# Attention sums moved by DMA in the projection's layout, instead of transposed on TensorE

## The reference

```python
scores = jnp.einsum('bhid,bhjd->bhij', q, k) * scale        # 16 heads of 16 features
scores = jnp.where(causal, -jnp.inf, scores)
attn = jax.nn.softmax(scores, axis=-1)
out = jnp.einsum('bhij,bhjd->bhid', attn, v)
out = jnp.transpose(out, (0, 2, 1, 3)).reshape(b, n, d)
return out @ proj_w.T + proj_b
...
x = x + _layernorm(_L0_attn_ref(_layernorm(x, axis=-1), ...), axis=-1)
x = x + _layernorm(_L0_ffn_ref(_layernorm(x, axis=-1), ...), axis=-1)
```

## Time and profile before

| | us |
|---|---|
| median of 3 runs | 1443.12 (1441.19 to 1446.45) |
| the profiled execution's own time | 1444.75 |
| span of its instructions | 1442.9 |
| PE busy | 1320.8 (92%) |
| DVE busy | 1070.2 (74%) |
| ACT busy | 872.5 (60%) |
| POOL busy | 603.3 (42%) |
| mean granted TensorE clock | 0.957 |

### The profile page before, as it was taken

The page is one execution under the profiler, slowest core; times in us unless marked ns, Lnnn a source line. Parts: engine busy times, 40 slices in busy tenths (PEclk is TensorE's granted clock), DMA queues, the critical chain, the costliest instruction groups (busy, mean ns, idle before and its releaser), DMA issues.

```text
span 1442.9 us, 30280 instructions
## 1 busy us (share of the span) xinstructions
PE 1320.8 (92%) x12592; PEld 609.8 (42%) x12592; DVE 1070.2 (74%) x1800; ACT 872.5 (60%) x1200; POOL 603.3 (42%) x521
## 2 busy tenths in 40 slices
PE   4678999999999999999999999999999989999994
PEld 1323444444444444444444444444444433555441
DVE  4765777867777786877687778777788986647778
ACT  3214766657665766676677667766666767665451
POOL 5556482226534462446245634553411323222334
PEclk9768999989999999999999999999999999999997
DMA  4382453344435353544353435353454530212112
GB/s 157 100 148 91 75 122 87 60 91 75 104 60 119 68 111 61 119 76 104 60 119 75 104 60 120 75 105 60 93 72 61 108 91 2 74 48 84 59 45 101
DMA packets 79805, 124.21 MB, mean 86 GB/s; under 512 B 14006, under 2 KB 49972, under 8 KB 79668
## 3 DMA queue, kind: packets, MB, share of 16 engines
q1 hardware_dynamic: 79668, 122.28, 39.8%
HBM read 70.85 MB, written 50.33 MB: 84 GB/s over the span
## 4 chain that ended last, share of the span: by engine, by line
PE 65%; POOL 12%; ACT 9%; DVE 6%; issue 4%; DMA 3%; SPq 2%; DVEq 0%; ACTq 0%; POOLq 0%
PE PV L993 15%; PE RING L953 10%; PE RING L979 10%; ACT PB L1334 6%; PE MI L918 6%; PE RING L1051 4%; PE MI L1017 4%; POOL TA L749 2%; PE MI L928 2%; POOL TB L751 2%; PE RING L1044 2%; PE RING L1045 2%; PE RING L1035 2%; POOL PB L1404 2%; PE RING L960 2%
## 5 line engine op out<-in xcount | busy, mean ns | idle before, releaser
L1334 ACT ACTIVATE PB<-RING 128x1024 f32<-128x1024 f32 (+2 forms) x640 | 581.9, 939 | 291.7 <-PE RING L979 287.8
L1127 DVE TENSOR_REDUCE M<-RING 128x2 f32<-128x1024 f32 (+3 forms) x448 | 499.2, 1143 | 146.6 <-PE RING L960 73.1
L993 PE MATMUL PV<-PB,V 128*17 128x512 f32 (+3 forms) x3072 | 328.8, 507 | 6.8 <-POOL PB L1404 5.9
L953 PE MATMUL RING<-QK 48*128 48x512 f32 (+3 forms) x1536 | 300.2, 410 | 36.5 <-DVE M L1127 15.0
L1404 POOL TENSOR_SCALAR_AFFINE_SELECT PB<-PB 128x512 f32<-128x512 f32 x256 | 163.3, 641 | 390.4 <-ACT PB L1334 390.2
L979 PE MATMUL RING<-QK 50*128 50x512 f32 (+3 forms) x1536 | 280.7, 406 | 11.6 <-ACT PB L1334 7.0
L1127 DVE TENSOR_REDUCE MB<-RING 128x2 f32<-128x768 f32 (+2 forms) x192 | 197.4, 1042 | 70.9 <-PE RING L960 69.8
L953 PEld LDWEIGHTS RING<-QK 48*128 48x128 f32 x1536 | 149.1, 192 | 188.7 <-issue 65.4
L979 PEld LDWEIGHTS RING<-QK 50*128 50x128 f32 x1536 | 134.2, 189 | 175.7 <-ACT PB L1334 73.4
L960 PE MATMUL RING<-MASKK,MASKQ 64*128 64x64 bf16 x2048 | 122.7, 200 | 0.0
L918 PE MATMUL MI<-XT,WQ 128*32 128x512 f32 x896 | 114.4, 630 | 2.3 <-ACT EO L1307 1.6
(11 more groups left out here) (111 smaller groups left out, 1386.5 us busy)
## 6 DMA issues: line engine op xcount, KB each, us to landing
QK<-split_parts SPq DMA_DIRECT2D x372, 128.0 KB, 5.8
split_parts<-PARTS SPq DMA_DIRECT2D x64, 256.0 KB, 3.5
split_parts<-EO SPq DMA_DIRECT2D x64, 256.0 KB, 4.3
block_mid<-Y SPq DMA_DIRECT2D x16, 512.0 KB, 4.1
F_X<-block_mid SPq DMA_DIRECT2D x16, 512.0 KB, 5.7
X<-x SPq DMA_DIRECT2D x7, 1024.0 KB, 9.7
out<-F_Y SPq DMA_DIRECT2D x14, 512.0 KB, 2.9
QK<-NSROW SPq DMA_DIRECT2D x128, 8.0 KB, 1.9
```

Source lines behind the costliest of these rows:

```text
L953: ins = e.matmul(m[:, h, i, :], QK[g % 3][r, 0, k, 128 * t:128 * t + 128], QK[g % 3][r, 1, k, k0:k0 + n], start=True, stop=not open_end(g, s))
L993: ins = e.matmul(PV[32 * h:32 * h + 17, off:512], V[b % 2][:, j, 4 * (g % 4) + h, :], PB[(SLOTS * g + s) % 4][:, h, 0:n], start=(j == 0), ...
L1127: e.tensor_reduce(acc, ring(("max", g, s, u), pairs, n), AX.X, ALU.max).then_inc(v_max, 1)
L1334: e.activation(buf[:, :, pairs[0]:pairs[-1] + 1, :], ring(("score", g, s, u), pairs, n), ACT.Exp).then_inc(a_exp, 1)
```

## The change: what is multiplied, moved and ordered

Five things change together.

1. The values lie as blocks of 16 columns, ones, values of head 2i, values of head 2i+1, ones, and so on. `product` takes 32 of these columns: values beside ones. `PV` then holds, for each head, 16 rows of values and 16 equal rows of the sum. The first four key blocks of a sequence have two buffers (`VL`), the last four one (`VU`).
2. `ot`, `ot_out`, `att` and `att_out` are gone. A new SP step `att_load` (64 of them) copies by five DMAs from `OT` the value rows into `ATT[c]` and the sum rows into `SUM[c]`, at the partitions that the projection wants. After every second group `att_inverse` (DVE, 32 of them, 128x512) inverts `SUM[c]` in place and `att_scale` (POOL, 32 of them) multiplies `ATT[c]` by it.
3. `ot_copy` now waits until the DMAs of the `att_load` before it have landed, since `OT` is one tile. Values of the last four key blocks are written only after the last product of the sequence before.
4. The causal mask of a narrow `max` unit (at most 256 columns) is added to both head pairs at once: 4 mask products of 128 columns instead of 8 of 64.
5. The planner's due times come from a table `DUE` and a function `pace`, its model of SP's DMAs is finer, and `LAG`, `LEAD`, `LOAD` and `STAY` have new values.

The core of the diff:

```diff
-SLOTS, LAG, LEAD, LOAD = 12, 3, 15, 21
+SLOTS, LAG, LEAD, LOAD = 12, 3.95, 15.08, 20.76
+EACH, EVEN = 365, 0.5
...
+DUE = {"ln_stats": (-10.78, 5.44), "ln_dev": (-9.94, -0.47), "ln_rows": (-7.23, 5.21), "xt": (-5.06, 16.12),
...
+def pace(columns):
+
+    work = [[2 * len(u) * n + EACH for u in units(n)] for n in columns]
+    total, at, out = sum(map(sum, work)), 0, []
+    for w in work:
+        out.append([])
+        for x in w:
+            out[-1].append(EVEN * (at / total * SLOTS) + (1 - EVEN) * (len(out) - 1 + (len(out[-1])) / 2))
+            at += x
+    return out
...
-        return [("product", g, 3 if c == 0 else 11), ("ot", g - 1 + c, 1 - c)]
...
+        return [("product", g, 3 if c == 0 else 11), ("att_load", g - 1 + c, 1 - c)]
+    if what == "att_load":
+        g, c = at
+        return [("ot_copy", g, c), ("att_scale", (g // 2 - 1) // 2, c, (g // 2 - 1) % 2), ("proj", g // 4 - 1, c, 2)]
...
-SWITCH, LOAD_ROWS, STAY, SLACK = 200, 100, 1.5, 0
+SWITCH, LOAD_ROWS, STAY, SLACK = 200, 100, 1.67, 0
...
-            V = [sb(f"V{i}", [128, 8, 16, 17]) for i in range(2)]
...
+            VL = [sb(f"VL{i}", [128, 4, 25, 16]) for i in range(2)]
+            VU = sb("VU", [128, 4, 25, 16])
...
+                elif what == "att_load":
+                    g, c = at
+                    k, r0 = g % 4 // 2, 64 * (g % 2)
+                    w.wait_ge(a_ot, 2 * g + c + 1)
...
+                    for r, p0 in ((0, 16), (32, 80)):
+                        e.dma_start(ATT[c][r0 + r:r0 + r + 32, k, :], OT[p0:p0 + 32, :]).then_inc(s_att[c], 16)
+                    for r, p0, n in ((0, 0, 16), (16, 48, 32), (48, 112, 16)):
+                        e.dma_start(SUM[c][r0 + r:r0 + r + n, :], OT[p0:p0 + n, :]).then_inc(s_att[c], 16)
...
-                                           QK[g % 3][r, 1, k, k0:k0 + n], start=True, stop=not open_end(g, s))
...
+                                           QK[g % 3][r, 1, k, k0:k0 + n], start=(i == 0), stop=not open_end(g, s))
+                    if open_end(g, s):
+                        w.wait_ge(v_mask, 1)
+                        for z in range(2):
+                            for h in range(2):
+                                r = slice(64 * h, 64 * h + 64)
+                                ins = e.matmul(m[:, h, :, n - 128 + 64 * z:n - 64 + 64 * z], MASKQ[r, z, :],
+                                               MASKK[r, z, :].unsqueeze(1).to_broadcast([64, len(pairs), 64]),
+                                               start=False, stop=(z == 1))
...
-                        ins = e.matmul(PV[32 * h:32 * h + 17, off:512], V[b % 2][:, j, 4 * (g % 4) + h, :],
...
+                        n0 = 48 * (2 * (g % 4) + h // 2) + 32 * (h % 2)
+                        ins = e.matmul(PV[32 * h:32 * h + 32, off:512], v[:, n0:n0 + 32],
                                        PB[(SLOTS * g + s) % 4][:, h, 0:n], start=(j == 0), stop=(j == 4 * c + 3))
...
-                    e.reciprocal(RC[:, :, :].unsqueeze(3), v4[:, :, :, 16:17]).then_inc(v_rc, 1)
-                    w.wait_ge(v_rc, NTH["ot_out", g, c])
-                    h0 = 64 * (g % 4)
-                    e.tensor_tensor(AT[:, 4 * c:4 * c + 4, h0:h0 + 64].rearrange("p q (h d) -> p q h d", h=4),
-                                    v4[:, :, :, 0:16], RC[:, :, :].unsqueeze(3).to_broadcast([128, 4, 4, 16]),
-                                    ALU.mult).then_inc(o_mi["ot"], 1)
+                elif what == "att_inverse":
+                    b, c, k = at
+                    w.wait_ge(s_att[c], 80 * (4 * b + 2 * k + 2))
+                    e.reciprocal(SUM[c][:, :], SUM[c][:, :]).then_inc(v_inv, 1)
...
-                    w.wait_ge(p_mi["ot"], 2 * g + c)
+
+                    w.wait_ge(s_att[1 - c], 80 * (g + c))
                     e.activation(OT[:, :], PV[:, :], ACT.Copy).then_inc(a_ot, 1)
...
+                elif what == "att_scale":
+                    b, c, k = at
+                    w.wait_ge(v_inv, NTH["att_inverse", b, c, k])
+                    e.tensor_tensor(ATT[c][:, k, :], ATT[c][:, k, :], SUM[c][:, :], ALU.mult).then_inc(g_att, 1)
```

More of the change, by code:

```diff
@@ L85, in prep_times @@
         return [(-1000 + i, s) for i, s in enumerate(steps)]
[L86 to L89, removed]
+    at = []
@@ L120, in due_times @@
         if b >= 2:
-            at.append((PER * (b - 1) - 24, ("load_x", b)))
+            at.append((PER * (b - 1) + DUE["load_x"][0], ("load_x", b)))
+    scores = pace([width(s)[3] for s in range(SLOTS)])
     for g in range(NG):
+        maxes = pace([reach(g, s)[3] for s in range(SLOTS)])
         if g:
@@ L305, in forward_needs @@
     if what in ("f_load", "f_zero"):
-        return [("values_out", last, 6), ("send", last, 1, 0), ("send", last, 1, 1), ("residual", last - 1, 1, 2)]
+        return [("values_out", last, 6), ("send", last, 1, 0), ("send", last, 1, 1), *[("residual", last - 1, c, 2) for c in range(2)],
+                ("score", NG - 3, SLOTS - 1, 0)]
     if what == "f_fill":
@@ L367 @@
 for engine, names in (
-        ("PE", "xt qk values fold max chain_turn score product ot att proj f_turn f_u1 up down f_y"),
-        ("ACT", "ln_rows xt_out qk_out values_out chain_turn_out exp ot_copy att_out y_rows f_turn_out gelu q_out"),
-        ("DVE", "ln_stats ln_dev ln_shift max_out chain_a chain_b ot_out proj_out fold_weights fold_out y_stats y_dev"
+        ("PE", "xt qk values fold max chain_turn score product proj f_turn f_u1 up down f_y"),
+        ("ACT", "ln_rows xt_out qk_out values_out chain_turn_out exp ot_copy y_rows f_turn_out gelu q_out"),
+        ("DVE", "ln_stats ln_dev ln_shift max_out chain_a chain_b att_inverse proj_out fold_weights fold_out y_stats y_dev"
                 " y_shift f_zero f_weights f_stats f_rows f_u1_out f_y_out f_spread f_shift"),
-        ("POOL", "ln_pow select y_pow residual f_pow f_ypow"),
-        ("SP", "load_x send load_group shift store f_load f_fill f_rest f_next f_store")):
+        ("POOL", "ln_pow select att_scale y_pow residual f_pow f_ypow"),
+        ("SP", "load_x send load_group shift att_load store f_load f_fill f_rest f_next f_store")):
     TAKER.update(dict.fromkeys(names.split(), engine))
@@ L535, in order_of_work @@
         free[engine] = start + took
-        done[step] = start + took + LATE[engine]
+        if engine == "SP":
+            size, rate, late = MOVES[step[0]]
+            if step[0] == "load_group" and step[2] is not None:
+                size //= 2
+            moved = max(moved, start + 500) + size / rate
+            done[step] = max(start + took + late, moved + 1800)
+        else:
+            done[step] = start + took + LATE[engine]
         if step[0] in EMPTIES:
@@ L806, in sync @@
                     if b >= 3:
-                        w.wait_ge(g_res, NTH["residual", b - 3, 1, 2])
+                        w.wait_ge(g_res, max(NTH["residual", b - 3, c, 2] for c in range(2)))
                     e.dma_start(X[b % 3][:, :, :], x_rows[b]).then_inc(s_x[b % 3], 16)
```

160 lines of the change are left out of this document (74 added, 86 removed), and 3 rows, old and new, of the table DUE.

## The result

| | before | after |
|---|---|---|
| median on the same chip | 1442.41 us | 1520.57 us (1514.24 to 1527.05, 4 runs) |
| ratio | 1 | 1.053 (1.050 to 1.056) |
| span of the profiled execution | 1442.9 | 1522.6 |
| PE busy | 1320.8 | 1360.1 |
| DVE busy | 1070.2 | 1166.6 |

A forecast was written before the change was run, and what follows sets the result against it. PE was taken to bound the attention, though not purely. From 1444.75 us, - 61 (PE work) + 29 (inversion waits) - 6 (lag) gave 1407, forecast as 1405 since the runs' median lay 1.6 lower; range 1366 to 1443.

The forecast's parts named there:

- I let 0.8 of it through, 61 us: Attention: of 76 us taken off PE's list, 0.8 was to come off the span, 61 us.
- the 29 us for the inversion: PE's waits for bank pairs held up behind DVE's inversions: 0.9 us for each of 32, bounds 0 and 103.
- 32 stationary columns at nothing: PE's product steps: loading 32 columns instead of 17 was priced at zero, with 46 us as upper bound.
- The inversion's length, 3.2 us: DVE: one inversion of 512 elements was to take about 3.2 us, from the row for 16 elements.
- The wait of 2.1 us that I took as the worst: PE's units finding no free bank pair behind one inversion on DVE: 2.1 us at worst.
- The masks, 16 us: PE's narrow max units: masks added to both head pairs at once were to save 16 us, bounds 0 and 25.
- The tile `OT`: Copies to this tile were to wait little for DMAs, say under 20 us in all.
- rival D: Copies of `OT` waiting for DMAs become the bound, shown by 60 us or more of waits: 1469 us, chance 0.11.
- The plan at nothing, bounds - 20 and + 20: The planner's new due times, taken at nothing beyond the counted excursions, within 20 us either way.
- The lag, - 6: Products lagging 3.95 slots instead of 3: a quarter of PE's 23.1 us of load waits for selects back, 6 us.
- PE busy in the attention down by about 76 us: Sign to look for in the profile: PE's busy time in the attention falls by about 76 us.
- Rival B: Attention: freed PE time turns into waits, only 0.4 of 76 us comes through: 1442 us, chance 0.10.
- the divide: DVE's inversion as a full eight-fold divide, 1.3 us longer each, 42 us more: 1447 us, chance 0.06.

The follow-up runs named there:

- the changed kernel without the inversion's length: The changed kernel with the DVE inversion of the sums replaced by a multiplication of the same tile by a constant: 1476.92 us, ratio 1.026.
- the filler: Score products of slots 4 to 7 issued twice into the same place, here in the changed kernel: ratio 1.065 with it, 1.053 without.
- the told planner: The changed kernel with the planner's cost of the inversion set from 650 to 3350 ns: 1576.69 us, ratio 1.096.
- the four pieces: The changed kernel with each inversion split into four pieces of 128 columns, each planned at 900 ns: 1545.6 us, ratio 1.076.

## Why the prediction was wrong

The step that failed is the one that ends "I let 0.8 of it through, 61 us", with the bounds 0.4 and 1. The work left PE's list much as forecast (65 us by the stage's rows), but none of it came off the span. Without the 29 us for the inversion my sum reads 1376; the changed kernel without the inversion's length takes 1477. A share below nothing was outside my bounds, and it was where the answer lay: with three quarters of the transposing products left out and nothing else changed, the old flow got 1.1% slower. In the stage of the changed kernel the clock took 101 us more and PE's idle time 37 more. I read the clock of 0.95 in the earlier trace rows as a property of the stage. The runs show that it moves with PE's list and with the waits around it. The reason given, "PE stood still in 6% of the stage before, and waits for ACT and DVE will grow with their shares", has only the idle time in it.

Point by point:

- 32 stationary columns at nothing: right. At the full clock, and with no pause behind it, a product step of 512 queries takes 0.99 us to the start of the next step (median of 95) against 0.98 before (median of 154); 15 ns more for each of its 8 loads would have been 0.12.
- The inversion's length, 3.2 us: right, 3.35. Its price, 0.9 us each with the bounds 0 and 103 us in all: mis-sized. It is 39 us (1.2 each) in the new flow, inside the bounds, and 153 (4.8 each) in the old one, outside. The wait of 2.1 us that I took as the worst leaves out the slow stretch behind each pause, and it counts only the reductions and the bank pairs: at 704.07 above PE waits 3.30 us for the chain, which also stands behind the inversion. The loads of `chain_turn` wait 27.3 us in the changed kernel, 17.0 without the inversion's length and 11.0 before.
- The masks, 16 us: about 12 as work, nothing clear of noise as time.
- The tile `OT`: "under 20 us in all" was the mark, and 13.2 were measured, far from the 60 of rival D.
- The plan at nothing, bounds - 20 and + 20: - 11 in the old flow, inside; - 71 (1.103 to 1.053) in the new one, far outside. That a plan is worth more where there is less slack is my reading, and no run isolates it.
- The lag, - 6: loads waiting for selects read 17.9 us for `VL` and 3.3 for `VU`, 21.2 together, against 23.1. It gave 2. In the old flow with the new plan they read 13.7.
- "PE busy in the attention down by about 76 us": this mark failed, and it was the one to show the mistake. Busy rose by 37 in the stage while the work fell by 65.

Rival B, "the freed PE time turns into waits", 1442, was the nearest in kind and had 0.10. It stops at no gain, because it has no clock in it. The slower side of my chances hung on `OT` and on the divide.

What stays open: which pattern of pauses brings the clock down. It isn't their sum alone: the changed kernel is idle for 107 us of the stage and loses 148 to the clock, and with the filler it is idle for 111 and loses 100. Open too is what else in the new flow, beside the missing work, takes the clock from 0.960 to 0.909, and why the told planner and the four pieces got worse.

## What to carry to other kernels

Read PE's busy time as work plus what the clock costs, by stage times (1 - granted clock), before pricing anything on PE. Where short pauses are frequent, work taken off PE can lower the clock and cost time (1.1% here), and useless products can be nearly free (- 4 to 17 us for 59 us of them); so a change to PE's list has a price on both sides of nothing, and the cheap test is to leave the work out, or to issue it twice, before rewriting the flow. Keep long single instructions off the engine whose small results PE waits for.

## What the runs showed of the hardware

A small DVE operation on SBUF can stretch to the end of a POOL operation beside it. DVE's timeline of the changed kernel:

```profile
744.35 2.31 DVE L1193 TENSOR_SCALAR NS<-M 128x32 fp32r<-128x32 f32 x1
746.70 0.19 DVE L1199 SCALAR_TENSOR_TENSOR NS<-M,NS 128x32 fp32r<-128x32 f32 x1
```

and POOL's:

```profile
744.24 2.39 POOL L802 TENSOR_TENSOR TB<-EO,SIN 128x1024 f32<-128x1024 f32 x1
746.70 1.32 POOL L805 TENSOR_TENSOR EO<-TA,TB 128x512 f32<-128x512 f32 x1
```

The operation of L1193 takes 0.18 us at 702.67. Here it starts 0.11 us after POOL's, ends with it, and takes 2.31. The Trainium skill, "SBUF — State Buffer", section "Who interferes with whom", says that the two engines share a pair of ports by an exclusive lock that one instruction holds to its end; the trace agrees, with 2.31 us in place of 0.18. So POOL's 32 multiplications by the inverse (41 us) aren't only beside DVE's work: the one at 702.69 meets the chain at 702.88, which takes 1.13 us. These stretches lie in the chain that PE waits for.

The inversion runs at 348 ns for 32 elements, 931 for 128 and 3346 for 512: 6.1 to 6.3 ns an element, so the estimate from 16 elements held at 32 times the size.
